# Second attention's keys: projected once and stacked by twelve transfers within SBUF

## What is computed

```python
x = x + xattn0(layernorm(x), ctx)      # 8 heads of 64
x = x + experts(layernorm(x))          # 8 experts, the 2 best per token, silu(x W1) * (x W2) @ W3
x = x + xattn1(layernorm(x), ctx)      # 16 heads of 8, with biases
x = x + ffn1(layernorm(x))             # three layers of +-1 weights

# xattn1
q = split_heads(x @ Wq + bq)
k = split_heads(context @ Wk + bk)
v = split_heads(context @ Wv + bv)
scores = jnp.einsum('bhqd,bhkd->bhqk', q, k) * scale
attn = jax.nn.softmax(scores, axis=-1)
out = jnp.einsum('bhqk,bhkd->bhqd', attn, v)
```

## Time and profile before

| | before |
|---|---|
| median of 3 runs, us | 253.0 (252.68, 253.0, 255.15) |
| profiled execution: its own time, us | 254.9 |
| its span, us | 253.1 |
| instructions | 5075 |
| busy: PE / DVE / ACT / POOL, us | 233.8 / 173.5 / 127.6 / 62.9 |
| granted TensorE clock, mean of the span | 0.953 |

### The profile page before, as it was taken

One profiled execution on the slowest core, in us unless ns is written; L12 is line 12 of the kernel. 1 busy time (PEld: TensorE's weight loads), 2 busy tenths in 40 slices (PEclk: granted clock), 3 DMA queues, 4 the chain that ended last, 5 costly groups with the idle time before them and its releaser, 6 DMA issues.

```text
span 253.1 us, 5075 instructions
## 1 busy us (share of the span) xinstructions
PE 233.8 (92%) x1834; PEld 192.1 (76%) x1834; DVE 173.5 (69%) x433; ACT 127.6 (50%) x298; POOL 62.9 (25%) x103
## 2 busy tenths in 40 slices
PE   8969888898999999999999999799999999689993
PEld 7347677797877898898898888586778887467782
DVE  0799988777767966556656669855678883378862
ACT  2644769779574722322331342432455657446741
POOL 3262396040400330311319102320000007220200
PEclk9998999999999999999999999955699999899999
DMA  6940000000000020120120000000000000000002
GB/s 198 223 124 1 3 25 21 0 3 0 3 0 0 4 63 22 40 62 13 52 62 0 23 0 1 0 3 0 1 3 3 3 0 3 0 3 0 1 3 83
DMA packets 11245, 6.62 MB, mean 26 GB/s; under 512 B 2772, under 2 KB 10904, under 8 KB 11224
## 3 DMA queue, kind: packets, MB, share of 16 engines
q1 hardware_dynamic: 11224, 6.33, 9.3%
HBM read 5.81 MB, written 0.52 MB: 25 GB/s over the span
## 4 chain that ended last, share of the span: by engine, by line
PE 71%; DVE 13%; ACT 7%; issue 4%; DMA 2%; POOL 2%; SPq 0%; DVEq 0%
PE ps L429 9%; PE ps L610 9%; PE ps L782 9%; PE ps L431 8%; PE ps L430 8%; PE ps L688 4%; ACT probs L883 3%; PE ps L520 3%; PE ps L701 3%; PE ps L500 3%; DMA x_sb<-in_x 2%; PE ps L729 2%; PE ps L425 2%; PE ps L436 2%; PE ps L714 2%
## 5 line engine op out<-in xcount | busy, mean ns | idle before, releaser
L932 ACT ACTIVATE kT<-ps 128x512 f32<-128x512 f32 x32 | 19.1, 597 | 41.9 <-PE ps L431 41.8
L610 PEld LDWEIGHTS ps<-w,kT 128*128 128x128 f32 x256 | 30.5, 192 | 0.7
L610 PE MATMUL ps<-w,kT 128*128 128x128 f32 x256 | 31.0, 275 | 0.0
L1244 DVE TENSOR_TENSOR kT<-ps,kT 128x512 f32<-128x512 f32 x32 | 21.8, 689 | 11.1 <-PE ps L431 8.8
L429 PE MATMUL ps<-xT_hi,w_hi 128*128 128x512 f32 x64 | 26.7, 417 | 0.7 <-issue 0.6
L431 PE MATMUL ps<-xT_hi,w_lo 128*128 128x512 f32 x64 | 25.2, 393 | 0.0
L430 PE MATMUL ps<-xT_lo,w_hi 128*128 128x512 f32 x64 | 25.0, 391 | 0.0
L1251 DVE SCALAR_TENSOR_TENSOR x_sb<-ps,comb,x_sb 128x128 f32<-128x128 f32 x64 | 18.0, 343 | 8.6 <-PE ps L610 8.5
L1342 DVE TENSOR_REDUCE probs<-ps 128x8 f32<-128x1024 f32 x16 | 19.6, 1225 | 6.0 <-PE ps L688 6.0
L883 ACT ACTIVATE probs<-ps,negmax 128x128 f32<-128x128 f32 x64 | 22.6, 418 | 1.8 <-DVE negmax L1169 1.8
L373 POOL TENSOR_TENSOR w_hi<-w_raw,zero 128x512 fp32r<-128x512 f32 x8 | 8.3, 1039 | 51.5 <-DMA w_raw<-in_L_ffn_W 37.2
(11 more groups left out here) (193 smaller groups left out, 538.8 us busy)
## 6 DMA issues: line engine op xcount, KB each, us to landing
w_raw<-in_L_ffn_W SPq DMA_DIRECT2D x16, 128.0 KB, 2.2
w<-in_L_ffn_W SPq DMA_DIRECT2D x8, 128.0 KB, 2.1
x_sb<-in_x SPq DMA_DIRECT2D x1, 512.0 KB, 5.8
out<-qo SPq DMA_DIRECT2D x2, 256.0 KB, 2.4
ctx_sb<-in_ctx SPq DMA_DIRECT2D x1, 384.0 KB, 3.4
w_raw<-in_L_xattn_Wq SPq DMA_DIRECT2D x1, 256.0 KB, 5.9
wo<-in_L_xattn_Wo SPq DMA_DIRECT2D x1, 256.0 KB, 5.7
k_i<-in_L_ffn_k SPq DMA_DIRECT2D x1, 256.0 KB, 3.7
```

Source lines behind the costliest of these rows:

```text
L610: ins = pe.matmul(ps[:, 4 + slot, k * C:(k + 1) * C], uT[:, slot, c, k * P:(k + 1) * P], w3[:, buf, c, :], start=(c == 0), stop=(c == NH - 1))
L932: act.activation(silu[:, c, :], ps[:, c, :], ACT.Silu).then_inc(b_silu, 1)
L1244: dve.tensor_tensor(uT[:, slot, c, :], ps[:, 2 + c, :], silu[:, c, :], ALU.mult).then_inc(b_u, 1)
```

## The change

`k1_keys(t)` now projects the keys once, without repetition, with three matmuls of 512 columns for each half, both ahead of the experts' loop. ACT copies the result as high part (`k1_high`, into `k1_hi`), DVE subtracts for the rest (`k1_low`, into `k1_lo`), both in the space of `h_a`. SP then writes the slots of `k_st`, 32 rows of 1024 values at a time, for four groups and three slots: twelve transfers of 128 KB within SBUF. The slots are interleaved now: row 4d + p of a head's 32 is channel d of slot p, which is why a transfer writes every fourth row. The fourth slot, and zeros elsewhere, are laid down before by one POOL copy of 128x4096 elements from a mask column (`k1_fill`). Masks, the layout of the query weights and `top_w` follow the new order. The last `k1_keys` behind the loop is replaced by `keep_clock(3, M0)`.

```diff
@@ sync
                 load_down(buf, buf)
+
+            sp.wait_ge(k1_fill, 1)
+            sp.wait_ge(k1_h, NT)
+            sp.wait_ge(k1_l, NT)
+            for g in range(NG):
+                for p, made in ((0, k1_hi), (1, k1_lo), (2, k1_hi)):
+                    sp.dma_start(f32(k_st[p::NS, g, :]), f32(made[32 * g:32 * g + 32, :])).then_inc(k1_st, 16)
             with sp.Fori(1, E // 2) as i:
@@ gpsimd
-            split_repeated(wk1, wk1_hi, wk1_lo)
+            chain(pool.tensor_copy(wk1_hi[:, 0:C], wk1[:, :]))
+            pool.tensor_tensor(wk1_lo[:, 0:C], wk1[:, :], f32(wk1_hi[:, 0:C]), ALU.subtract).then_inc(split_w1, 1)
...
             pool.wait_ge(a_wo, NB)
+            pool.wait_ge(masks, 9)
+            pool.tensor_copy(k_st[:, :, :].rearrange("p g n -> p (g n)"),
+                             is_lo[:, 1:2].to_broadcast([P, NG * NB * P])).then_inc(k1_fill, 1)
 
             with pool.Fori(1, E // 2) as i:
@@ tensor
-            def k1_keys(i, m):
-                for k in range(2):
-                    gs, cols = slice((2 * m + k) * P, (2 * m + k + 1) * P), bass.ds(i * 2 * P, 2 * P)
-                    ins = split3(ps[:, M0 + m, k * 2 * P:(k + 1) * 2 * P], wk1_hi[:, gs], wk1_lo[:, gs],
-                                 ctxT_hi[:, cols], ctxT_lo[:, cols])
-                ins.then_inc(k1_ps, 1)
+            def k1_keys(t):
+                sl = slice(t * TG, (t + 1) * TG)
+                split3(ps[:, M0 + t, :], wk1_hi[:, 0:C], wk1_lo[:, 0:C], ctxT_hi[:, sl], ctxT_lo[:, sl]).then_inc(k1_ps, 1)
...
-            k1_keys(0, 0)
+            k1_keys(0)
             keep_clock(3, 4)
             pe.wait_ge(ln_lo, 2 * NT)
             gate_logits(1)
+            k1_keys(1)
             b_hidden(1, 0, 1, (0,))
...
                 b_hidden(i * 4 + 3, 1, 1)
-                k1_keys(i, 1)
                 b_down(i * 4 + 2, 0, 1, i)
...
-                k1_keys(i + 1, 0)
...
-            k1_keys(NP - 1, 1)
+            keep_clock(3, M0)
             keep_clock(4, M0)
@@ scalar
-                act.activation(part[:, m, :], ps[:, M0 + m, :], ACT.Copy, scale=sign[:, 1:2]).then_inc(k1_part, 1)
+            def k1_high(t):
+                act.wait_ge(k1_ps, t + 1)
+                act.activation(k1_hi[:, t * TG:(t + 1) * TG], ps[:, M0 + t, :], ACT.Copy).then_inc(k1_h, 1)
@@ vector
+            def k1_low(t):
+                dve.wait_ge(k1_h, t + 1)
+                sl = slice(t * TG, (t + 1) * TG)
+                dve.tensor_tensor(k1_lo[:, sl], ps[:, M0 + t, :], f32(k1_hi[:, sl]), ALU.subtract).then_inc(k1_l, 1)
...
-            k1_stack(0, 0)
+            for t in range(NT):
+                k1_low(t)
```

More of the change, by code:

```diff
@@ L167, in program @@
         v_a = qo[:, :, :, :].rearrange("p z a (b h d) -> p (z a b) h d", h=H1, d=VW)
+        k1_hi, k1_lo = (h_a[:, 0, 2 * i:2 * i + 2, :].rearrange("p k n -> p (k n)") for i in range(2))
         q_all = h_c[:, :, :, :].rearrange("p s k n -> p (s k n)").rearrange("p (g n) -> p g n", g=NG)
@@ L189, in program @@
         M0 = 6
-        NK1 = 2 * NP
+        NK1 = 16 * NG * 3
         LN_BANK = ((M0, 5), (4, M0 + 1), (3, M0 + 1), (0, M0 + 1))
@@ L225, in program @@
             sem("b_" + n) for n in ("hi", "lo", "h", "g", "silu", "u", "y", "acc"))
-        k1_ps, k1_part, k1_st, v1_ps, v1_ok = (sem(n) for n in ("k1_ps", "k1_part", "k1_st", "v1_ps", "v1_ok"))
+        k1_ps, k1_h, k1_l, k1_fill, k1_st, v1_ps, v1_ok = (
+            sem(n) for n in ("k1_ps", "k1_h", "k1_l", "k1_fill", "k1_st", "v1_ps", "v1_ok"))
         c_q_ps, c_part, c_q, c_v, c_s, c_max, c_w, c_qa, c_st, c_exp, c_o, c_ov, c_ovT, c_rs, c_norm, \
@@ L235, in stacked @@
         def stacked(ap):
-            return ap[:, :].rearrange("c (h p d) -> c h p d", p=NS, d=D1)
+            return ap[:, :].rearrange("c (h d p) -> c h p d", p=NS, d=D1)
         def repeated(ap):
@@ L361, in _ @@
             pool.wait_ge(k0_ps, NC0 * NT)
-            split_repeated(wk1, wk1_hi, wk1_lo)
+            chain(pool.tensor_copy(wk1_hi[:, 0:C], wk1[:, :]))
+            pool.tensor_tensor(wk1_lo[:, 0:C], wk1[:, :], f32(wk1_hi[:, 0:C]), ALU.subtract).then_inc(split_w1, 1)
             pool.wait_ge(split_w1, 1)
-            chain(pool.memset(stacked(f32(wk1_hi))[CK:CK1, :, NS - 1, 0:1], 1.0))
             pool.memset(f32(ones_r[:, :]), 1.0).then_inc(split_w1, 1)
@@ L932, in b_silu_step @@
                     act.activation(silu[:, c, :], ps[:, c, :], ACT.Silu).then_inc(b_silu, 1)
-            def k1_signed(i, m):
-                act.wait_ge(k1_ps, i * 2 + (m + 1))
-                act.activation(part[:, m, :], ps[:, M0 + m, :], ACT.Copy, scale=sign[:, 1:2]).then_inc(k1_part, 1)
+            def k1_high(t):
+                act.wait_ge(k1_ps, t + 1)
+                act.activation(k1_hi[:, t * TG:(t + 1) * TG], ps[:, M0 + t, :], ACT.Copy).then_inc(k1_h, 1)
             def gate_copy(t):
@@ L948, in _ @@
             b_silu_step(1)
-            act.wait_ge(masks, 10)
-            k1_signed(0, 0)
+            for t in range(NT):
+                k1_high(t)
             act.wait_ge(g_d, 1)
@@ L957, in _ @@
                 b_silu_step(i * 4 + 3)
-                k1_signed(i, 1)
                 b_silu_step(i * 4 + 4)
                 b_silu_step(i * 4 + 5)
-                k1_signed(i + 1, 0)
             b_silu_step(2 * E - 2)
@@ L970, in c_query_signed @@
                     act.wait_ge(c_q, n - 1)
-                else:
-                    act.wait_ge(k1_st, NK1 - 1 + n)
+                elif n == 0:
+                    act.wait_ge(masks, 10)
                 act.activation(part[:, n % 2, :], ps[:, q_bank(n), :], ACT.Copy,
@@ L976, in _ @@
             ln_hi_copy(2, 0)
-            k1_signed(NP - 1, 1)
             for n in range(NG):
@@ L1143, in stack_masks @@
                 dve.wait_ge(const_ok, 4)
-                dve.tensor_scalar(bit_i[:, 0:1], row_i[:, :], 4, 1, ALU.logical_shift_right, ALU.bitwise_and).then_inc(masks, 1)
-                dve.tensor_scalar(bit_i[:, 1:2], row_i[:, :], 3, 3, ALU.logical_shift_right, ALU.bitwise_and).then_inc(masks, 1)
+                dve.tensor_scalar(bit_i[:, 0:1], row_i[:, :], 1, 1, ALU.logical_shift_right, ALU.bitwise_and).then_inc(masks, 1)
+                dve.tensor_scalar(bit_i[:, 1:2], row_i[:, :], 0, 31, ALU.logical_shift_right, ALU.bitwise_and).then_inc(masks, 1)
                 dve.tensor_scalar(bit_i[:, 2:3], row_i[:, :], 0, 1, ALU.logical_shift_right, ALU.bitwise_and).then_inc(masks, 1)
@@ L1149, in stack_masks @@
                 dve.wait_ge(masks, 8)
-                dve.tensor_scalar(is_lo[:, 1:2], is_lo[:, 1:2], 1.0, None, ALU.is_equal).then_inc(masks, 1)
+                dve.tensor_scalar(is_lo[:, 1:2], is_lo[:, 1:2], float(NS - 1), None, ALU.is_equal).then_inc(masks, 1)
                 dve.wait_ge(masks, 9)
@@ L1305, in _ @@
                 b_gate(q + 3, 1)
-                k1_stack(i, 1)
                 b_add(q + 2, 0, e + 1, 0, q + 3)
@@ L1310, in _ @@
                 b_gate(q + 5, 1)
-                k1_stack(i + 1, 0)
             q = 2 * E - 4
@@ L1324, in _ @@
             ln_low(2, 0)
-            k1_stack(NP - 1, 1)
             dve.wait_ge(b_acc, q + 6)
@@ L1340, in c_top @@
                 dve.wait_ge(c_s, 2 * b + a + 1)
-                top = top_w[:, b % 2, :, :].rearrange("p g (r m) -> p r g m", r=4)[:, 2 * a:2 * a + 2, :, 3 * D1]
+                top = top_w[:, b % 2, :, :].rearrange("p g (r m) -> p r g m", r=4)[:, 2 * a:2 * a + 2, :, NS - 1]
                 dve.tensor_reduce(top, ps[:, S_BANK:S_BANK + 2, :].rearrange("p r (g k) -> p r g k", g=NG), X, ALU.max,
```

## The result

| | before | after |
|---|---|---|
| median of the undisturbed runs, us | 253.0 (252.68 to 255.15) | 262.25 (260.83 to 263.95) |
| profiled execution: time / span, us | 254.9 / 253.1 | 262.16 / 260.3 |
| instructions | 5075 | 4975 |
| granted clock, mean of the span | 0.953 | 0.944 |

The ratio is 1.034 (95% interval 1.028 to 1.039): the change makes the kernel 3.4% slower, where 257.5 was forecast. In each group of runs on the chip some executions ran at the lower clock for most of their second half (some 274 to 289 us); they are left out of every median and ratio here, and of the profiles of `e1`, `e4` and `e9`, which were such executions, only rows ahead of 160 us are used.

What follows compares the result with a forecast made beforehand. PE was taken to bound the experts' loop, DVE the part ahead of it. Late weights +6.4, removed projections -3.6 and low clock +1.7 gave +4.5 on 253.0: 257.5 us, forecast 255.5 to 260, full range 254 to 262.5.

Steps and rivals of the forecast that it cites:

- The fill, its length and its hold: Ahead of the loop: POOL's fill takes 3.7 us from 79.95 and holds DVE's L1157, +2.3 us for all that follows.
- The queue: SP issues twelve transfers ahead of expert 2's weight load; PE waits 4.4 us, hidden block at 100.8 instead of 94.38, +6.4.
- Twelve issues at 0.45 us, 5.4 us: On SP from 90.1, ahead of expert 2's load: issuing the twelve transfers lasts until 95.5.
- I add nothing: Expert 2's load behind the twelve transfers: their data in flight, 0 to 1 us later, was counted as no delay.
- The clock behind the wait: After PE's wait for expert 2: 3.4 us of dense matmuls at half rate lose 1.7 us.
- The loop's gain: In the experts' loop: five removed key projections behind expert 2's wait give -3.6 us; later pairs take 18.2 us.
- Nothing behind the loop: Behind the loop, before the scores: the wait goes over query work that stays, so nothing is gained there.
- The time it was set on: Whole kernel: the +4.5 us was set on the median of 253.0, giving 257.5; about 259.4 in a run like the profiled one.
- the cheap edition: Rival, ahead of the loop: DVE not held by the fill, issues of 0.37 us; 253.2, or 254.9 with the clock; chance 0.13.
- The long stretch of low clock behind the scores: Rival, 164 to 182 us: the stretch does not come back, 5 us less, 252.5; chance 0.12.
- Slow transfers: Rival: the twelve transfers move at half the rate (+5), or the fill takes 8.3 us (+4.6); 262 to 262.5; chance 0.13.

Runs made afterwards that it cites:

- e1: Changed kernel with the weight loads of experts 2 and 3 issued ahead of the twelve transfers on SP; 256.5 us, ratio 1.006 to the kernel before.
- e4: Changed kernel with loads of experts 2 and 3 ahead of the transfers, and masks and fill in the first 8 us; 251.0 us, ratio 0.985.
- e9: Kernel before plus four within-SBUF transfers of 128 rows of 4 KB (2 MB) ahead of SP's loop; 262.4 us in one run.
- e5: Kernel before plus one POOL fill of 128x4096 into an unused buffer ahead of POOL's loop; 262.5 us in two runs against 253.8.
- e3: Changed kernel with transfers of 32x512 instead of 32x1024, leaving half of the keys out; 263.3 us in one run.
- e10: Kernel before plus twelve transfers of 32 rows of 4 KB to neighbouring partitions, ahead of SP's loop; 263.6 us in one run.
- e6: Kernel before plus twelve transfers of 128 KB to every fourth row, between areas not in use, ahead of SP's loop; 264.5 us, ratio 1.039.
- e7: Changed kernel with early fill, second-half keys projected after expert 0's last hidden block, key splits and transfers behind the engines' loops; 249.5 us, ratio 0.983.

## Why the prediction was wrong, step by step

- *The fill, its length and its hold*: right. 3.7 us from 79.95 was forecast, 3.60 from 79.61 came; the subtraction was to start at 85.90 and started at 85.92; both `k1_low` were to be done at 90.05 and were at 90.03. In one point the reason was too narrow: the operation held was the one ahead of L1157's counterpart (L1158, 3.57 us), which has one tensor source and a column of scalars, while L1157's own counterpart, with two tensors, ran behind it in 0.34; e1 and e5 show a plain copy (1.55 and 1.37 us instead of 0.35) held as well. So operations on two SBUF tensors are not the only ones held.
- *The queue*: the mechanism was right, and this is the step that failed, in one term. **Twelve issues at 0.45 us, 5.4 us**: they took 0.64 each, 7.95 to the load's issue, +2.55. The 0.45 was read off weight loads and carried over to another kind of transfer without an upper bound from above. e3 and e10 rule out bytes and spread as its cause, e6 shows the same step in the kernel before. The load took 3.3 us instead of 2.8 (+0.5): "I add nothing" for data in flight was that much too low, as e3 with half the bytes is back at 2.7. Together expert 2 started at 103.89, not at 100.8: +3.1.
- *The clock behind the wait*: 1.7 forecast, 1.9 measured, in part by luck. The forecast had 3.4 us at the low level, all under dense matmuls; measured are 6.8 us (101.3 to 108.1), of which 2.6 lay in the wait and cost nothing. In e6 they were 10.2 us and cost 2.8. The clock also fell behind expert 1's wait of 2.20 us, which made that expert's hidden block 1.6 us longer; that lay under the wait for expert 2 and cost nothing.
- *The loop's gain*: 3.6 us behind that point, 3.6 measured; a later pair of experts takes 18.21 us (113.23 to 131.44) against 19.64 before (102.50 to 122.14), as forecast.
- *Nothing behind the loop*: -0.7. The new low stretch in the queries (3.4 us long) costs 1.5 us; against it the long one is shorter (13.7 us, 176.4 to 190.0, against 17.1, 164.6 to 181.6), and one of 3.4 us from 218.8 has no counterpart after. That fits the sign; no run prices these stretches one by one.
- With these sizes the sum is +9.5 + 1.9 - 3.6 - 0.7 = +7.2 us, instead of +4.5. That is what the two profiled spans differ by.
- *The time it was set on*: I put the difference on the median of 253.0, 1.9 below the profiled execution of before. The profile after lies at its own median (262.16 and 262.25), so the medians differ by 9.2 while the spans differ by 7.2. The rest, some 2 us, is in no row, and it may be noise: the interval of the ratio (1.028 to 1.039) is 7.2 to 9.9 us, and the kernel before took 255.2, 253.8 and 255.6 (one run) in the other groups. By the mean clocks (0.946 to 0.966 in undisturbed runs of before, 0.953 in its profiled one, 0.935 to 0.947 after) more low clock in the median run of the changed kernel is possible too. Neither is shown.
- *The rivals*: the cheap edition fell: DVE was held, and an issue step took 0.64, not 0.37. The long stretch of low clock behind the scores came back, 176.4 to 190. "Slow transfers" had the right size (262 to 262.5), but named the bytes, and e3 excludes these for all but 0.6 us; what was slow is issuing. That the measured 262.25 lies at this rival's price is luck.

## What to carry to other kernels

When a batch of transfers goes into a queue, count the issues at the step of its own kind of transfer, and look at what is queued behind them: in e6 twelve issues of 0.64 us cost 9.2 us ahead of the weight loads, with the low clock behind the wait, and in e7 nothing behind the last one. Fewer and wider transfers were cheaper here (e9, +4.7 in the loop for more bytes), though their third and fourth issue took longer. And a long GpSimd operation is not free because GpSimd is idle: place it where VectorE has nothing on the critical path, and check what GpSimd does right behind it, since in e1 and e5 each further GpSimd operation held a further one on VectorE.

## What the runs showed of the hardware that I had not expected

- An issue of a within-SBUF transfer takes 0.59 to 0.60 us on SP, a step of 0.64, with 64 or 128 KB in 32 rows, to neighbouring or spread rows, and the first two of 512 KB in 128 rows are much the same (0.53 and 0.60); weight loads of 128 KB have steps of 0.46.
- Where 512 KB transfers follow each other at that step, the third and fourth issue take 0.79 and 1.22 us, and the next load's issue 0.92.
- A VectorE operation of 2x128 elements with one tensor source took 3.57 us beside a GpSimd copy, and a copy of 2x384 elements 1.37 to 1.55 us instead of 0.35 beside a GpSimd subtraction.
